# Moving both attention products to the end of slot 1, with four probability buffers and the output's store on SP

## The reference

```python
# route: (16, 64, 128, 128); H = 8 heads of D = 16; FF = 512; EPS = 1e-5
q = (route @ wq + bq).reshape(b_, r_, k_, H, D)      # k and v in the same way
scores = jnp.einsum('brkhd,brnhd->brknh', q, k) / D ** 0.5
attn = jax.nn.softmax(scores, axis=3)
out = jnp.einsum('brknh,brnhd->brkhd', attn, v).reshape(b_, r_, k_, m_)
out = out @ wo + bo
x = _layernorm(route + out, ln1_g, ln1_b)
ff = jax.nn.relu(x @ w1 + b1) @ w2 + b2
return _layernorm(x + ff, ln2_g, ln2_b)
```

## Time and profile before

| what | value |
|---|---|
| median of three runs | 4191.73 us |
| profiled execution, device time | 4193.59 us |
| its span | 4191.8 us |
| granted PE clock, mean | 0.992 of full speed |
| PE / PEld busy | 98% / 84% |
| DVE / ACT / POOL busy | 87% / 83% / 88% |
| DMA engines' mean busy share | about 0.7 in every slice |
| traffic | 755.76 MB moved, mean 180 GB/s |

### The profile page before, as it was taken

The page is one execution under the profiler, slowest core; times in us unless marked ns, Lnnn a source line. Parts: engine busy times, 40 slices in busy tenths (PEclk is TensorE's granted clock), DMA queues, the critical chain, the costliest instruction groups (busy, mean ns, idle before and its releaser), DMA issues.

```text
span 4191.8 us, 150532 instructions
## 1 busy us (share of the span) xinstructions
PE 4090.8 (98%) x49930; PEld 3541.1 (84%) x49930; DVE 3650.1 (87%) x9740; ACT 3494.4 (83%) x5890; POOL 3708.3 (88%) x3864
## 2 busy tenths in 40 slices
PE   6999999999999999999999999999999999999997
PEld 5888888888888888888888888888888888888886
DVE  6888888888888888888888888888888888888885
ACT  4888888888888888888878888888888888888886
POOL 4889998998899999989989889998999998988987
PEclk7999999999999999999999999999999999999999
DMA  7777777777777777777767777777777777777772
GB/s 150 183 179 189 183 185 185 183 188 180 187 181 189 179 188 186 182 185 183 186 173 180 188 180 186 185 182 184 184 190 181 188 182 184 185 182 185 181 187 76
DMA packets 1466634, 755.76 MB, mean 180 GB/s; under 512 B 644736, under 2 KB 1432960, under 8 KB 1465856
## 3 DMA queue, kind: packets, MB, share of 16 engines
q1 hardware_dynamic: 1158672, 605.66, 58.6%
q10 hardware_dynamic: 307184, 140.40, 12.2%
HBM read 202.51 MB, written 134.22 MB: 80 GB/s over the span
## 4 chain that ended last, share of the span: by engine, by line
PE 40%; DVE 18%; issue 12%; ACT 10%; POOL 8%; SPq 5%; DMA 3%; ACTq 3%; DVEq 1%; POOLq 0%
PE bankB L705 6%; DVE max_sb L559 5%; PE bankC L705 5%; PE s_ps L719 5%; POOL rs L332 5%; PE bankC L682 5%; PE oT_ps L746 5%; PE sT_ps L733 5%; PE bankB L682 3%; DMA x_blocks<-in_x 3%; ACT n_sb L459 3%; DVE st L576 3%; PE bankA L759 3%; SPq L247 2%; ACT m_sb L417 2%
## 5 line engine op out<-in xcount | busy, mean ns | idle before, releaser
L559 DVE TENSOR_REDUCE max_sb<-s_ps 128x8 f32<-128x1024 f32 x1024 | 1218.4, 1190 | 7.1 <-PE s_ps L719 5.8
L429 ACT ACTIVATE prob_sb<-sT_ps 128x1024 f32<-128x1024 f32 x1024 | 1046.3, 1022 | 153.3 <-PE sT_ps L733 110.1
L288 POOL TENSOR_TENSOR parts<-rest_sb,parts 128x512 bf16<-128x512 f32 x512 | 584.4, 1163 | 187.4 <-ACT parts L396 177.6
L719 PEld LDWEIGHTS s_ps<-stack 96*128 96x128 bf16 x8192 | 465.1, 98 | 278.5 <-issue 152.9
L719 PE MATMUL s_ps<-stack 96*128 96x128 bf16 x8192 | 641.0, 222 | 25.7 <-DVE max_sb L559 16.3
L459 ACT ACTIVATE n_sb<-z_sb,shift,rs 128x128 f32<-128x128 f32 x1024 | 422.1, 482 | 264.0 <-POOL shift L334 264.0
L733 PE MATMUL sT_ps<-stack 99*128 99x128 bf16 x8192 | 629.0, 219 | 4.3 <-ACT prob_sb L429 4.1
L746 PE MATMUL oT_ps<-prob_sb,v_ones 128*32 128x128 f32 x16384 | 555.1, 276 | 5.0 <-ACT prob_sb L429 3.3
L705 PE MATMUL bankB<-w_sb,h_sb 128*128 128x128 f32 x4096 | 526.9, 282 | 16.7 <-ACT h_sb L408 15.4
L746 PEld LDWEIGHTS oT_ps<-prob_sb,v_ones 128*32 128x32 f32 x16384 | 417.1, 110 | 128.7 <-issue 51.1
L733 PEld LDWEIGHTS sT_ps<-stack 99*128 99x128 bf16 x8192 | 503.9, 98 | 7.1 <-ACT prob_sb L429 5.7
(11 more groups left out here) (75 smaller groups left out, 8401.0 us busy)
## 6 DMA issues: line engine op xcount, KB each, us to landing
stack<-parts SPq DMA_DIRECT2D x3072, 128.0 KB
x_blocks<-in_x SPq DMA_DIRECT2D x1024, 64.0 KB, 2.4
n_mem<-n_sb SPq DMA_DIRECT2D x1024, 64.0 KB
n_blocks<-n_mem SPq DMA_DIRECT2D x256, 256.0 KB, 3.5
out<-out_sb ACTq DMA_DIRECT2D x256, 256.0 KB, 4.1
x_sb<-in_x ACTq DMA_DIRECT2D x255, 256.0 KB, 3.1
stack<-max_parts ACTq DMA_DIRECT2D x768, 8.0 KB
h_sb<-in_L_conv_w SPq DMA_DIRECT2D x1, 256.0 KB, 2.9
```

Of the source, the lines that this page charges most:

```text
L288: pool.tensor_tensor(parts[:, r % 2, 3 * c + LO], rest_sb[:, c], parts[:, r % 2, 3 * c + MID], ALU.subtract).then_inc(lo_split, 1)
L429: act.activation(prob_sb[:, s % 2], sT_ps[:], ACT.Exp, scale=float(D) ** -0.5).then_inc(exp_done, 1)
L559: dve.reduce_max(max_sb[:, (r - lag) % 2, :, s], s_ps[:].rearrange("p (h k) -> p h k", h=H), AX.X).then_inc(max_done, 1)
L719: ins = pe.matmul(s_ps[:, h * P:(h + 1) * P], stack[0:PROD, (r - lag) % 4, 0, h, tok], stack[0:PROD, (r - lag) % 4, 1, h, tok], start=True ...
```

## The change

On PE both attention halves now stand at the end of slot 1, after `down`, both for the group of lag 4; the first writes `bankA`, the second `oT_ps`. The half at the end of slot 3 is gone. `prob_sb` has four buffers in place of two. On DVE `turn_out(0)` and `invert(0)` move from the first part of the step to the place ahead of `row_max(2)`, `turn_out(1)` behind it, and the max chain moves from ahead of `row_max(3)` to the place between `turn_x` and `row_max(0)` of the next step (lag 3 in place of 2). On ACT the three max rows move with it, among the Relus and exponentials of slots 0 and 1; `xT_hi` moves behind the second exponential; the v copy moves between the two middle parts. On POOL the sum `xb_sb` takes the place of `xT_lo`, which moves behind the scale and shift. The output's store moves from ACT to the end of SP's step. Two scratch tiles go (`x1g_sb`, `mg_sb`); their operations write in place.

```diff
@@ buffers
-        prob_sb = sb("prob_sb", [P, 2, H * P])
+        prob_sb = sb("prob_sb", [P, SEQS, H * P])
@@ SP, end of the step
+                if live(t, r, 9):
+                    sp.wait_ge(out_ready, upto(t, r, 9, plus=1))
+                    sp.dma_start(out_g[t + (r - 9)], out_sb[:, (r - 9) % 2]).then_inc(out_stored[(r - 9) % 2], DMA)
@@ POOL, behind x1 (in place of xT_lo, which now stands behind shift)
+                if live(t, r, 1):
+                    pool.wait_ge(x_loaded[(r - 1) % 2], upto_dma(t, r, 1))
+                    if (v := upto(t, r, 5, plus=1)) is not None:
+                        pool.wait_ge(z_done, v)
+                    pool.tensor_tensor(xb_sb[:, (r - 1) % 4], x_sb[:, (r - 1) % 2], each_seq(bo_row),
+                                       ALU.add).then_inc(xb_done, 1)
@@ ACT, exponentials
-                    if (v := upto(t, r, lag, per=2, plus=s // 2)) is not None:
+                    if (v := upto(t, r, lag, per=2, plus=s // 2 - 1)) is not None:
                         act.wait_ge(pv_done, v)
-                    act.activation(prob_sb[:, s % 2], sT_ps[:], ACT.Exp, scale=float(D) ** -0.5).then_inc(exp_done, 1)
+                    act.activation(prob_sb[:, s], sT_ps[:], ACT.Exp, scale=float(D) ** -0.5).then_inc(exp_done, 1)
@@ ACT, step
+                exponentials(t, r, 0)
+                if live(t, r, 7):
+                    relu(t, r, 7, 2)
+                if live(t, r, 3):
+                    act.wait_ge(max_parts_made, upto(t, r, 3, plus=1))
+                    max_row(t, r, HI)
+                if live(t, r, 7):
+                    relu(t, r, 7, 3)
+                if live(t, r, 3):
+                    max_row(t, r, MID)
+                exponentials(t, r, 1)
+                if live(t, r, 3):
+                    max_row(t, r, LO)
                 if live(t, r, 0):
                     act.wait_ge(x_turned, upto(t, r, 0, plus=1))
                     ...
                     act.activation(xT_parts[:, HI], xT_sb[:], ACT.Copy).then_inc(xT_hi, 1)
-                if live(t, r, 9):
-                    act.wait_ge(out_ready, upto(t, r, 9, plus=1))
-                    act.dma_start(out_g[t + (r - 9)], out_sb[:, (r - 9) % 2]).then_inc(out_stored[(r - 9) % 2], DMA)
                 ...
                 if live(t, r, 0):
                     mid_part(t, r, 0)
-                    mid_part(t, r, 1)
-                if live(t, r, 6):
-                    relu(t, r, 6, 0)
-                if live(t, r, 2):
-                    act.wait_ge(max_parts_made, upto(t, r, 2, plus=1))
-                    max_row(t, r, HI)
-                if live(t, r, 6):
-                    relu(t, r, 6, 1)
-                if live(t, r, 2):
-                    max_row(t, r, MID)
                 if live(t, r, 0):
                     act.wait_ge(v_done, upto(t, r, 0, plus=1))
                     ...
-                if live(t, r, 2):
-                    max_row(t, r, LO)
+                if live(t, r, 0):
+                    mid_part(t, r, 1)
+                if live(t, r, 6):
+                    relu(t, r, 6, 0)
+                if live(t, r, 6):
+                    relu(t, r, 6, 1)
@@ DVE, turn_out reads bank A for half 0
-                              oT_ps[:].rearrange("p (s f b q) -> p s f b q", s=2, f=2, b=4)).then_inc(oT_turned, 1)
+                              (A, oT_ps)[half][:].rearrange("p (s f b q) -> p s f b q", s=2, f=2, b=4)).then_inc(oT_turned, 1)
@@ DVE, step, between turn_x and row_max(0)
-                if live(t, r, 4):
-                    turn_out(t, r, 0)
+                if live(t, r, 3):
+                    mT, max_rest = oT_ps[0:H * SEQS, 0:P], oT_ps[0:H * SEQS, P:2 * P]
+                    dve.wait_ge(maxT_done, upto(t, r, 3, plus=1))
+                    ...
                 row_max(t, r, 0)
@@ DVE, step, around row_max(2)
                 if live(t, r, 4):
-                    turn_out(t, r, 1)
+                    turn_out(t, r, 0)
+                    invert(t, r, 0)
                 row_max(t, r, 2)
                 if live(t, r, 4):
+                    turn_out(t, r, 1)
+                if live(t, r, 4):
                     invert(t, r, 1)
                 if live(t, r, 0):
                     rest(t, r, 0)
                     rest(t, r, 1)
-                if live(t, r, 2):
-                    ... (the max chain, lag 2)
                 row_max(t, r, 3)
@@ PE, attend
+                if half == 0:
+                    pe.wait_ge(v_copied, upto(t, r, 4, plus=1))
+                    if (v := upto(t, r, 5, plus=1)) is not None:
+                        pe.wait_ge(z_done, v)
+                else:
+                    pe.wait_ge(max_parts_made, upto(t, r, 3, plus=1))
+                    if (v := upto(t, r, 4, per=2)) is not None:
+                        pe.wait_ge(oT_turned, v)
@@ PE, step
                 if live(t, r, 4):
-                    attend(t, r, 4, 1)
+                    attend(t, r, 0)
+                    attend(t, r, 1)
...
-                if live(t, r, 3):
-                    ...
-                    attend(t, r, 3, 0)
```

More of the change, by code:

```diff
@@ L334, in step @@
                     pool.tensor_tensor(shift[:], minus_m[:], rs[:], ALU.mult).then_inc(shift_done, 1)
+                if live(t, r, 0):
+                    pool.wait_ge(xT_hi, upto(t, r, 0, plus=1))
+                    if (v := upto(t, r, 0)) is not None:
+                        pool.wait_ge(k_done, v)
+                    pool.tensor_tensor(xT_parts[:, REST], xT_sb[:], xT_parts[:, HI].bitcast(F32),
+                                       ALU.subtract).then_inc(xT_lo, 1)
                 if live(t, r, 6):
@@ L398, in max_row @@
             def max_row(t, r, part):
-                act.dma_start(stack[PROD + part:PROD + part + 1, (r - 2) % 4, 0],
+                act.dma_start(stack[PROD + part:PROD + part + 1, (r - 3) % 4, 0],
                               max_parts[:, part]).then_inc(max_rows_loaded, DMA)
@@ L500, in _ @@
             act.wait_ge(consts_made, N_MADE)
-            iterate(act, step, 1, LEAD, LAST, 9)
+            iterate(act, step, 1, LEAD, LAST, 8)
         @block.vector
@@ L591, in step @@
                     turn_x(t, r)
-                if live(t, r, 4):
-                    turn_out(t, r, 0)
+                if live(t, r, 3):
+                    mT, max_rest = oT_ps[0:H * SEQS, 0:P], oT_ps[0:H * SEQS, P:2 * P]
+                    dve.wait_ge(maxT_done, upto(t, r, 3, plus=1))
+                    if (v := upto(t, r, 3, per=MAXROWS * DMA)) is not None:
+                        dve.wait_ge(max_rows_loaded, v)
+                    dve.tensor_scalar(max_parts[:, HI], mT, -1.0, None, ALU.mult).then_inc(max_hi, 1)
+                    dve.wait_ge(max_hi, upto(t, r, 3, plus=1))
+                    dve.scalar_tensor_tensor(max_rest, mT, -1.0, max_parts[:, HI],
+                                             ALU.mult, ALU.subtract).then_inc(max_rest_made, 1)
+                    dve.wait_ge(max_rest_made, upto(t, r, 3, plus=1))
+                    dve.tensor_copy(max_parts[:, MID], max_rest).then_inc(max_mid, 1)
+                    dve.wait_ge(max_mid, upto(t, r, 3, plus=1))
+                    dve.tensor_tensor(max_parts[:, LO], max_rest, max_parts[:, MID],
+                                      ALU.subtract).then_inc(max_parts_made, 1)
                 row_max(t, r, 0)
@@ L628, in step @@
                 if live(t, r, 4):
+                    turn_out(t, r, 0)
+                    invert(t, r, 0)
+                row_max(t, r, 2)
+                if live(t, r, 4):
                     turn_out(t, r, 1)
-                row_max(t, r, 2)
                 if live(t, r, 4):
@@ L735, in scores_turned, with attend @@
                     ins.then_inc(sT_done, 1)
-            def attend(t, r, lag, half):
-                pe.wait_ge(exp_done, upto(t, r, lag, per=SEQS, plus=2 * half + 2))
-                pe.wait_ge(v_copied, upto(t, r, lag, plus=1))
-                if (v := upto(t, r, lag, per=2, plus=half)) is not None:
-                    pe.wait_ge(oT_turned, v)
+            def attend(t, r, half):
+                pe.wait_ge(exp_done, upto(t, r, 4, per=SEQS, plus=2 * half + 2))
+                if half == 0:
[3 more added lines that the diff above has]
+                    else:
+                        pe.wait_ge(v_copied, upto(t, r, 0))
+                else:
+                    pe.wait_ge(max_parts_made, upto(t, r, 3, plus=1))
+                    if (v := upto(t, r, 4, per=2)) is not None:
+                        pe.wait_ge(oT_turned, v)
                 for k in range(2):
```

53 lines of the change are left out of this document (14 added, 39 removed).

## The result

The changed kernel took 4273.51 us (median of four runs, 4267.99 to 4276.71), the kernel before in the same session 4188.16. The ratio is 1.0201, with a 95% interval of 1.0183 to 1.0220. That is 85 us, against the 55 between the 4191.73 that stood at the time and the 4247 that was forecast. The sign and the mechanism held; the size was too small by 30 us, or 0.1 us a step; the time lies at the upper end of the likeliest case, 4215 to 4275.

What follows compares the result with a forecast made beforehand. PE set a 15.76 us floor, with a landing loop of 15.67 close behind. The loop grows by 0.55 to 16.22, the step from 16.03 to 16.25: 250 x (16.25 - 16.03) = 55 us, so 4247 us; 8-in-10 range 4145 to 4315.

Steps and rivals of the forecast that it cites:

- the likeliest case: Forecast case with the loop at 16.15 to 16.3 a step: 4215 to 4275 us, chance 0.48.
- The loop through the landing: One-step loop from `turn_x` through DVE, POOL, ACT, SP and the block landing: 15.67 us before, 16.22 after.
- The term for the chain: On DVE ahead of `row_max(0)`, four max operations (1.15) replace `turn_out(0)` (0.60): the loop grows by 0.55.
- The 0.03 added for other hold-ups: Added to the 16.22 us loop for steps that something else holds up; stated as 0.03 to 0.08.
- the rival of the landing: Max rows leave ACT before the loads, the landing shrinks and PE wins: 4169 or 4139 us; chance of a gain 0.22.
- 0.25 a step with a chance of 0.10 as a rival: The store ahead of SP's writes lengthens the landing: step 16.5, 4311 us; chance 0.10.
- The rival's own sign: For the rival that the store lengthens the landing: the last load lands later than 3.0 us on average.
- The store goes exactly into that idle stretch: SP idles before the writes of n, so the store's one added issue (0.4 to 0.6 us) costs zero.
- the sign: PE's second scores wait for `max_sb`, 100 to 180 us in the changed profile.
- That is most of the 0.27: Steps where the landing releases `turn_x` (57 of 220, averaging 16.14) explain most of the 0.27 above PE's 15.76.
- POOL's cover: POOL's 0.5 us wait for `mv`, with `mv` 0.55 later, covers the later low part (0.60): zero, at most 0.1.
- a late POOL: Rival: the low part's lateness adds 0.1 a step, 4274 us, POOL waiting for nothing at `minus_m`; chance 0.10.

Runs made afterwards that it cites:

- e1: The changed kernel with SP's four loads of the next blocks issued ahead of the four writes of n: 4143.9 us, ratio 0.9882.
- e9: The changed kernel with the max chain moved from behind `turn_x` to ahead of it, at the end of DVE's step: 4151.1 us, ratio 0.9922.
- e3: The changed kernel with the output's store back on ACT, at the head of ACT's step: 4247.3 us, ratio 1.0135.
- e10: The kernel of e9 with the output's store back on ACT: 4109.7 us, ratio 0.9825.
- e12: The kernel of e10 with `xb_sb` on POOL moved behind the first normalise: 4087.8 us, ratio 0.9763.
- e7: The kernel before with `turn_out(0)` moved behind the first norm's aggregation: 4165.2 us, ratio 0.9946.
- e2: The kernel before with SP's block loads issued ahead of the writes of n: 4174.5 us, ratio 0.9954.
- e4: The kernel before with one more DVE transpose (0.60 us, into an unread tile) between `turn_out(0)` and `row_max(0)`: 4316.5 us, ratio 1.0304.
- e8: The changed kernel with POOL's `xb_sb` back behind the first normalise: 4270.0 us, ratio 1.0195.
- e11: The kernel before with one more DVE transpose (0.6 us, into an unread tile) ahead of `add_y(t, r, 1)`, where DVE waits for PE: 4187.9 us, ratio 1.0005.

## Why the prediction was right, and where not

**The loop through the landing.** Right, and shown: e1 opens it at SP, e9 shortens it on DVE, and both take the changed kernel below the one before. The term for the chain, +0.55, measured +0.56 in the table.

**The size.** The forecast had 16.25 for the step and the trace has 16.38. The missing 0.13 is in the terms of the sum: the loop of before was 15.71 with its slack taken off, not 15.67; `row_max(0)`, `z_sb` and scale and shift grew by 0.04; first write to landing grew by 0.06, against zero in the forecast; landing to `turn_x` averages 0.20, not 0.18. The 0.03 added for other hold-ups went into this. Seen from the experiments, nearly all of the miss is the store: without it (e3) the step is 16.27 and the time 4247.3. That these meet the forecast so closely is in part luck, as a loop 0.04 longer than summed and pieces that grew by 0.04 were offset by the 0.03 and by a landing that was 0.05 shorter (2.65). The 4139 in the rival of the landing should be 4141 (4193.6 - 250 x 0.21); nothing hangs on it.

**The output's store.** Mis-sized. The prediction took zero and kept 0.25 a step with a chance of 0.10 as a rival. e3 measures 0.10 a step, 26 us of the 85; e9 against e10 gives 41. The rival's own sign, a last landing later than 3.0, did not come (2.75). The argument "The store goes exactly into that idle stretch" looked at SP's time for this one issue. What the store lengthens is what comes behind it: against e3, first write to first load 0.06, last landing 0.10, less 0.05 in the issues of the loads. The rule of the Trainium skill (DMA: Bandwidth & Descriptors, queues, rings and completion order) that descriptors are consumed in ring order fits, but no run shows the mechanism inside the rings: that part is argued.

**PE.** Right in size: 15.76 to 15.53 (forecast 15.55), worth nothing behind the loop. PE's wait for `max_sb` came out longer than the sign had it, 197.9 us against 100 to 180, as the step did. e12 against e7 gives 77 us for the kernels with and without the halves side by side, but they differ in more than that; the 0.23 a step, 58 us, is read from the PE timeline.

**What the 0.27 of before was.** Wrong. The step "That is most of the 0.27" failed. Of its 67 us, taking the landing out of the loop gave back 15 (e2), and taking `turn_out(0)` out of both loops 25 (e7), which is a lower bound for the two together; the rest is not shown to be either's. A share of steps that end late at one wait is no proof that they would have been early without it. The prediction also missed the second loop through ACT's norms, which is 0.1 longer than the landing's, and which only e4 brought out.

**POOL, max rows.** POOL's cover held in the changed kernel (e8), as forecast. The sign that the prediction gave for a late POOL, no wait at `minus_m`, did show (7.9 us), but it was a poor sign: `xb_sb` in front of it took the wait over. ACT's issues between Relus cost nothing visible there; PE's wait ahead of `down`, summed over the steps from the PE timeline, is 1 us in the changed kernel and 19 before.

**The rival of a shorter landing** fell: the last landing took 2.75 on average, not 2.4 or less, though the max rows had left its window. With the store on ACT as before (e3) it took 2.65 against 2.70, so their leaving shortened the mean landing by 0.05, if that is what did it.

## What to carry to other kernels

In a software pipeline that is written by hand, look for loops that close in one step: start at an operation that waits for a DMA, follow who waits for whom until the next issue of the same DMA, and add up starts, not durations. An operation moved between the landing and the next issue costs its time, less the slack that the loop still had, even on an engine with idle time (0.49 of 0.60 in e4). The max chain just ahead of the wait gave back 122 us (e9), and a transpose in a gap elsewhere cost nothing measurable (e11). When a loop is removed, look again at the edits that were free while it ruled: they may be the next bound (e8 against e12).

## What the runs showed of the hardware

From the last of four loads' landing to the start of the instruction that waits for it is 0.18 us, in 213 of 220 steps of the changed kernel. Moving a 256 KB store from ACT's queue to the place ahead of writes and loads on SP's lengthened the stretch from the first write to the last landing by 0.12 us a step in the changed kernel (7.00 against 6.88 in e3) and by 0.33 with the max chain ahead of `turn_x` (7.31 in e9 against 6.98 in e10), while the DMA engines' mean share stood between 0.71 and 0.76 in all four. Four dependent operations on 32 x 128 elements of 0.24 to 0.29 us each take 1.12 to 1.15 in a row, up to the start of the next operation.
